# VectorE's low halves of v, cut into single turns and spread over step 0, in a masked attention kernel

## The chip, the cores and the metric

The kernel runs on one core of a Trainium2 chip. The metric is the device time of one execution in microseconds (us); lower is better. The engines are TensorE (PE in the profile), VectorE (DVE), ScalarE (ACT), GpSimd (POOL) and SyncE (SP), which here only issues transfers.

## The reference

With M = N = 6144 and D = 128, x goes through a layer norm and a relu, is multiplied by a 128x128 weight and by the transposed nodes, is masked by an adjacency matrix, goes through a softmax over the 6144 nodes, and the result weighs the nodes:

```python
h = jnp.maximum(_layernorm(x, axis=-1), 0.0)
anchor_adj = jnp.einsum('md,de,ne->mn', h, weight, input)
scores = jnp.where(adj > 0, anchor_adj, NEG_PAD)
atten = jax.nn.softmax(scores / TEMPERATURE, axis=1)
x = x + atten @ input
```

## The kernel before, in words

The rows of x are done in 48 tiles of 128. One step t of the main loop does the second half of the work of tile t and, interleaved with it, the scores of tiles t+1 and t+2. A tile's 6144 columns are cut into 12 "turns" of 512. For each turn k, the probabilities are transposed and split in a high and a low fp16 half, and `product(t, par, k, at)` multiplies them with `v`, the nodes, which are held as two fp16 halves too: `v[:, block, 0, :]` is the high half and `v[:, block, 1, :]` the low one. A turn has four blocks of 128 nodes (PER_TURN = 4), and `v` has 48 blocks.

`v` is made once. The high halves are made by ScalarE (L474) in four parts of 12 blocks, that is of three turns each (PART = 12 blocks, PART_TURNS = 3). The low half is `nodes * scale - high`. Parts 0 and 3 (turns 0 to 2 and 9 to 11) are made by GpSimd, each by two instructions (L397, then L400), and parts 1 and 2 (turns 3 to 5 and 6 to 8) by VectorE with one `scalar_tensor_tensor` each (L649), which reads the raw nodes and the high half, both in SBUF. VectorE's two fall in step 0, at the middle of its first and of its second cycle.

A step has three cycles z, each of four turns. Every engine runs a program of its own, written out by hand, and waits on semaphores. The orders that matter here are these.

- TensorE, in each cycle: transposes of turn 4z (L795, function `turn`), six score matmuls of one 1024-column chunk (L777), transposes of turn 4z+1, products of turns 4z and 4z+1 (L819 and L821, eight matmuls a turn), six more score matmuls, in cycle 0 the transposes of h of tile t+2 (L770), and products of turns 4z+2 and 4z+3. In step 0 the score chunks are chunks 4 and 5 of tile 1, then 0 to 3 of tile 2.
- VectorE, in each cycle: two low halves of turns that were transposed by DMA (`lo_d`, L611), the low half of turn 4z (`lo_p`, L605), the masking and the running maximum of one score chunk (`mask`, L583), `lo_p` of turn 4z+1, in cycle 1 also the statistics of x (L562, L565), and a second `mask`. Behind the second one in cycle 0 come the low half of h (`lo_h`, L569) and `find_max` (L591, L593).
- ScalarE: the high half of the transposed turn (`hi_p`, L487), an exponential of 1024 columns (L446), two of 512 (L455) and their high halves (`hi_d`, L467), some of which wait for DMA transposes.
- GpSimd: for every 2048 columns of the adjacency one `present` (L375) and one `absent` (L384), and per tile three small operations for the layer norm (L354, L357, L363). Its part 3 of v (L397, L400) lies between the absent of tile 2's first columns and the present of its second.

A turn's transposes go into one of three PSUM banks; `turn` waits on `turn_freed` until the low half that read that bank is done. So turn 5 waits for the first `lo_d` of cycle 1. Product k needs the low halves of v for its turn in step 0 only; every later step uses them as they are.

Of the kernel before, what the change touches and what calls it, by code (L numbers as in the profile page):

```python
# [5 lines left out]
def gnn_masked_attention_kernel(  # L6
# [29 lines left out]
    PER_TURN = TURN // P  # L36
# [9 lines left out]
    PART = BLOCKS // PARTS  # L46
    PART_TURNS = TURNS // PARTS
# [28 lines left out]

    EARLY = 4

    V_POOL = (0, 3)
    V_VECTOR = (1, 2)  # L80
    HEAD = 3
    TAIL = 5

# [9 lines left out]
    with ctx:  # L93
# [6 lines left out]
        def sem(name):  # L100
            return ctx.enter_context(nc.semaphore(name))
# [110 lines left out]
        v_hi_done = sem("v_hi_done")  # L212
        v_lo_done = sem("v_lo_done")
# [25 lines left out]
        def evac(t, n, at=None):  # L239


            if at == LAST and n >= 8:
                n -= 2
            return t * TURNS + (n + 1 + EARLY)

        def high(t, n, at=None):

            return t * TURNS + (n - CYCLE + 3 + EARLY) if at == LAST and n >= 0 else evac(t, n)
# [9 lines left out]
        def has(at, ahead):  # L258
            return at is None or at + ahead < TILES
# [82 lines left out]
        def _(pool):  # L342
# [48 lines left out]
            def v_lo_pool(n):  # L391

                i = V_POOL[n]
                blocks = slice(i * PART, (i + 1) * PART)
# [164 lines left out]
        def _(dve):  # L559
# [13 lines left out]
            def mask(u, s, j):  # L573
                if isinstance(u, int) and u == 1 and j // PER_CONV == 1:
                    dve.wait_ge(absent_early_done, 1)
                elif isinstance(u, int) and (u == 0 or u == 1 and j < PER_CONV):
                    dve.wait_ge(absent_done, u * CONVS + (j // PER_CONV + 1))
                else:
                    dve.wait_ge(absent_done, u * CONVS + j // PER_CONV)
                dve.wait_ge(scores_made, u * SCORES + (j + 1))  # L580
                dve.sem_inc(dve_waited, 1)
                c, part = j // PER_CONV, j % PER_CONV
                nc.vector.tensor_tensor_reduce(  # L583
                    out=probs[:, s, j * SCORE:(j + 1) * SCORE],
                    in0=ps_s[j % 2][:, :], in1=absent[:, c, part * SCORE:(part + 1) * SCORE],
                    scale=1.0, scalar=LOWEST, op0=ALU.subtract, op1=ALU.max,
                    accum_out=chunk_max[:, s, j:j + 1]).then_inc(masked, 1)
# [8 lines left out]
            def lo_p(t, k, at):  # L596
                n, p = k, P_TURN[k]
                if at == LAST:
                    dve.wait_ge(turned, t * P_TURNS + (p + 1))
                    dve.wait_ge(pv_done, t * TURNS + (MULTIPLIED[p - BANKS] + 1 - (0 if p >= BANKS else TURNS)))  # L600
                    nc.vector.tensor_copy(pT_hi[:, p % BANKS, :], ps_t[n % BANKS][:, :]).then_inc(last_hi_done, 1)  # L601
                    dve.wait_ge(last_hi_done, p + 1)
                else:
                    dve.wait_ge(hi_done, evac(t, n, at))
                nc.vector.tensor_tensor(pT_lo[:, p % BANKS, :], ps_t[n % BANKS][:, :], pT_hi[:, p % BANKS, :],  # L605
                                        ALU.subtract).then_inc(turn_freed, 1)

            def lo_d(c, g, n, count):
                d = c + g
                dve.wait_ge(hi_done, count)  # L610
                nc.vector.tensor_tensor(split[:, d % BANKS, 1, :], ps_t[n % BANKS][:, :], split[:, d % BANKS, 0, :],  # L611
                                        ALU.subtract).then_inc(turn_freed, 1)
# [11 lines left out]
            def finish(u, s, free):  # L624
                dve.wait_ge(inv_done, u + 1)
                dve.wait_ge(x_res_in[s], loads(u, s))
                dve.wait_ge(pv_done, u * TURNS + TURNS)
                nc.vector.scalar_tensor_tensor(out=fin_a[:, s, :], in0=ps_o[:, 0:D], scalar=inv_sum[:, s, :],
                                               in1=x_res[:, s, :], op0=ALU.mult, op1=ALU.add)\
                    .then_inc(fin_a_done, 1)  # L630
                dve.wait_ge(fin_a_done, u + 1)
                if free:
                    dve.wait_ge(stored[s], loads(u - 2, s))
                nc.vector.scalar_tensor_tensor(out=fin[:, s, :], in0=ps_o[:, D:2 * D], scalar=inv_sum[:, s, :],
                                               in1=fin_a[:, s, :], op0=ALU.mult, op1=ALU.add)\
                    .then_inc(fin_done, 1)
# [5 lines left out]
                                               in1=yT_hi[:, cols], op0=ALU.mult, op1=ALU.subtract)\  # L642
                    .then_inc(y_lo_done, 1)

            def v_lo(i):
                dve.wait_ge(v_hi_done, i + 1)
                dve.wait_ge(scale_steps, 4)
                blocks = slice(i * PART, (i + 1) * PART)
                nc.vector.scalar_tensor_tensor(out=v[:, blocks, 1, :], in0=nodes_raw[:, blocks, :], scalar=scale,  # L649
                                               in1=v[:, blocks, 0, :], op0=ALU.mult, op1=ALU.subtract)\  # L650
                    .then_inc(v_lo_done, 1)
# [79 lines left out]
            mask(1, 1, 2)  # L731
            mask(1, 1, 3)

            def step(t, par, at):
                nxt = 1 - par
                if at != 0:
                    finish(t - 1, nxt, at is None or at > 2)
                for z in range(CYCLES):

                    ahead, c = ((0, 2), (0, 4), (1, 0))[z]  # L740
                    if has(at, ahead):
                        for g in range(2):
                            n = CYCLE * z - 2 + g
                            lo_d(c, g, n, high(t, n, at))
                    lo_p(t, CYCLE * z, at)
                    for q in range(2):
                        ahead, j = S_AT[CYCLE * z + 2 + q]
                        if has(at, ahead):
                            mask(t + ahead, (par + ahead) % 2, j)
                            if j == SCORES - 1:  # L750
                                if has(at, 2):
                                    lo_h(t + 2, par, ps_s[0])
                                find_max(t + ahead, (par + ahead) % 2)
                        if q == 0:
                            lo_p(t, CYCLE * z + 1, at)
                            if z == 1 and has(at, 3):
                                x_stats(t + 3, nxt)
                            if z == 2:
                                invert_sum(t, par)
                            if at == 0 and z < 2:  # L760
                                v_lo(V_VECTOR[z])

            steps(dve, step)
            finish(TILES - 1, (TILES - 1) % 2, True)

        @block.tensor
        def _(pe):
# [29 lines left out]
                made.then_inc(turned, 1)  # L797

            def product(t, par, k, at):
                if at == 0 and k % PART_TURNS == 0:  # L800
                    part = k // PART_TURNS
                    if part in V_POOL:
                        pe.wait_ge(v_lo_pool_done, V_POOL.index(part) + 1)
                    else:
                        pe.wait_ge(v_lo_done, V_VECTOR.index(part) + 1)
                if k in MULTIPLIED:
                    p = MULTIPLIED.index(k)
                    pe.wait_ge(turn_freed, evac(t, k - 2, at))
                    hi = [pT_hi[:, p % BANKS, b * P:(b + 1) * P] for b in range(PER_TURN)]
                    lo = [pT_lo[:, p % BANKS, b * P:(b + 1) * P] for b in range(PER_TURN)]  # L810
                else:
                    d = k // CYCLE * 2 + k % 2
                    pe.wait_ge(turned_in[d], t * 16 + 16)
                    hi = [pT_dma[:, d, b, :] for b in range(PER_TURN)]
                    lo = [pT_dma[:, d, PER_TURN + b, :] for b in range(PER_TURN)]
                area = ps_o
                for b in range(PER_TURN):
                    blk = k * PER_TURN + b
                    nc.tensor.matmul(area[:, 0:2 * D], hi[b], v[:, blk, :, :].rearrange("p s d -> p (s d)"),  # L819
                                     start=(blk == 0), stop=(blk == BLOCKS - 1), skip_group_check=True)  # L820
                    made = nc.tensor.matmul(area[:, 0:D], lo[b], v[:, blk, 0, :],  # L821
                                            start=False, stop=(blk == BLOCKS - 1), skip_group_check=True)
                made.then_inc(pv_done, 1)
# [112 lines left out]
```

## Time and profile before

| what | value |
|---|---|
| median of 3 executions | 939.33 us |
| lowest and highest | 935.38 and 939.46 us |
| the profiled execution's own time | 936.15 us |
| its span in the profile | 934.2 us |
| PE busy | 915.2 us (98%) |
| DVE busy | 814.7 us (87%) |
| ACT busy | 757.8 us (81%) |
| POOL busy | 656.7 us (70%) |

Busy time is that of the profiled execution, over its span. Matmuls overlap in the pipeline, so a busy PE does not mean one at its peak. Step 0 begins at about 41 us and ends at about 66 us of the span.

### The profile page before, as it was taken

How to read it: one execution, taken by the hardware profiler on the slowest of the kernel's cores; microseconds unless marked ns; L12 is line 12 of the kernel's file. 1: busy time of each engine (PE TensorE's matmuls, PEld its weight loads, DVE VectorE, ACT ScalarE, POOL GpSimd, SP SyncE). 2: the span in 40 equal slices, each digit the busy share in tenths (PEclk: the TensorE clock that was granted, in tenths of full speed). 3: DMA queues.
4: the chain of work that ended last, by engine and by line, in shares of the span. 5: the costliest groups of instructions: out<-in, count | busy, mean ns of one | idle time of the engine just before them, and what ended most of it. 6: DMA issues, size and time to landing. Idle time of an engine off the chain costs nothing.

```text
span 934.2 us, 25959 instructions
## 1 busy us (share of the span) xinstructions
PE 915.2 (98%) x7611; PEld 664.6 (71%) x7611; DVE 814.7 (87%) x1675; ACT 757.8 (81%) x1512; POOL 656.7 (70%) x443
## 2 busy tenths in 40 slices
PE   7989999999999999999999999999999999999997
PEld 4457777777777777777777777777777777777776
DVE  7888888888888889888888889888888888888886
ACT  6868788888888888888888888888888888888885
POOL 4999677767767776777677767776777677767710
PEclk9999999999999999999999999999999999999999
DMA  9799999999999999999999999999999999999955
GB/s 338 239 221 250 274 271 263 269 260 266 264 269 266 260 262 267 269 266 257 267 269 268 251 269 267 274 249 270 270 265 257 263 273 265 264 260 260 271 94 97
DMA packets 347401, 239.51 MB, mean 256 GB/s; under 512 B 308848, under 2 KB 327408, under 8 KB 328944
## 3 DMA queue, kind: packets, MB, share of 16 engines
q1 hardware_dynamic: 340176, 235.92, 97.2%
q10 hardware_dynamic: 7200, 3.28, 1.2%
q8 instruction: 13, 0.21, 0.1%
q14 instruction: 12, 0.10, 0.0%
HBM read 160.50 MB, written 3.15 MB: 175 GB/s over the span
## 4 chain that ended last, share of the span: by engine, by line
PE 93%; DVE 3%; DMA 2%; ACT 1%; issue 1%; DVEq 0%; SPq 0%; ACTq 0%
PE ps_s L777 38%; PE ps_o L819 26%; PE ps_t L795 13%; PE ps_o L821 13%; DMA pT_dma<-split 1%; DVE probs L583 1%; PE ps_t L838 1%; PE ps_s L848 1%; DVE pT_lo L605 1%; PE ps_s L770 1%; DMA nodes_raw<-in_L_gnn_input_dram 1%; DVE split L611 0%; DVE v L649 0%; ACT ps_t L455 0%; DVE pT_hi L601 0%
## 5 line engine op out<-in xcount | busy, mean ns | idle before, releaser
L583 DVE CUSTOM_DVE_ANT_0 probs<-ps_s,absent 128x1024 f32<-128x1024 f32 x288 | 351.6, 1221 | 80.6 <-PE ps_s L777 58.2
L384 POOL TENSOR_SCALAR absent<-present 128x2048 bf16<-128x2048 bf16 x143 | 299.5, 2094 | 79.3 <-DVE chunk_max L583 53.4
L375 POOL TENSOR_SCALAR present<-adj_i 128x2048 bf16<-128x2048 int32 x144 | 274.6, 1907 | 28.9 <-DMA adj_i<-in_adj_dram 23.8
L487 ACT ACTIVATE pT_hi<-ps_t 128x512 f16<-128x512 f32 x282 | 168.3, 597 | 113.9 <-PE ps_t L795 111.3
L455 ACT ACTIVATE ps_t<-probs,neg_max,exp_scale 128x512 f32<-128x512 f32 x288 | 222.9, 774 | 2.9 <-DVE neg_max L593 1.2
L777 PE MATMUL ps_s<-yT_hi,hT_hi 128*128 128x512 f16 x576 | 218.3, 379 | 1.1 <-DVE chunk_max L583 0.9
L777 PE MATMUL ps_s<-yT_lo,hT_hi 128*128 128x512 f16 x576 | 218.2, 379 | 0.0
L819 PE MATMUL ps_o<-v,pT_hi 128*128 128x256 f16 x1152 | 207.3, 274 | 5.1 <-DVE v L649 3.7
L819 PE MATMUL ps_o<-v,pT_dma 128*128 128x256 f16 x1152 | 205.6, 273 | 0.0
L605 DVE TENSOR_TENSOR pT_lo<-ps_t,pT_hi 128x512 f16<-128x512 f32 x288 | 196.9, 684 | 3.4 <-ACT pT_hi L487 3.2
L821 PE MATMUL ps_o<-v,pT_lo 128*128 128x128 f16 x1152 | 199.2, 220 | 0.0
L821 PE MATMUL ps_o<-v,pT_dma 128*128 128x128 f16 x1152 | 197.9, 219 | 0.0
L611 DVE TENSOR_TENSOR split<-ps_t,split 128x512 f16<-128x512 f32 x288 | 185.2, 682 | 5.2 <-ACT split L467 5.0
L467 ACT ACTIVATE split<-ps_t 128x512 f16<-128x512 f32 x288 | 162.2, 589 | 21.7 <-DMA pT_dma<-split 20.5
L795 PE MATMUL ps_t<-ident,probs 128*128 128x128 f32 x1152 | 175.9, 276 | 3.5 <-DVE split L611 3.5
L446 ACT ACTIVATE probs<-probs,neg_max,exp_scale 128x1024 f32<-128x1024 f32 x144 | 177.7, 1234 | 0.0
L777 PE MATMUL ps_s<-yT_hi,hT_lo 128*128 128x512 f16 x576 | 171.3, 379 | 0.0
L795 PEld LDWEIGHTS ps_t<-ident,probs 128*128 128x128 f32 x1152 | 128.7, 141 | 40.3 <-DVE split L611 20.4
L819 PEld LDWEIGHTS ps_o<-v,pT_hi 128*128 128x128 f16 x1152 | 113.1, 98 | 32.9 <-DVE v L649 4.4
L821 PEld LDWEIGHTS ps_o<-v,pT_lo 128*128 128x128 f16 x1152 | 113.1, 98 | 11.4
L819 PEld LDWEIGHTS ps_o<-v,pT_dma 128*128 128x128 f16 x1152 | 112.7, 98 | 11.5
L821 PEld LDWEIGHTS ps_o<-v,pT_dma 128*128 128x128 f16 x1152 | 112.7, 98 | 1.6
(72 smaller groups left out, 590.1 us busy)
## 6 DMA issues: line engine op xcount, KB each, us to landing
adj_i<-in_adj_dram SPq DMA_DIRECT2D x144, 1024.0 KB, 5.1
pT_dma<-split SPq DMA_TRANSPOSE x288, 3.4
nodes_raw<-in_L_gnn_input_dram SPq DMA_DIRECT2D x6, 512.0 KB, 7.0
x_res<-in_x_dram SPq DMA_DIRECT2D x48, 64.0 KB, 4.7
out_dram<-fin ACTq DMA_DIRECT2D x48, 64.0 KB, 2.9
x_ln<-in_x_dram SPq DMA_DIRECT2D x46, 64.0 KB, 4.9
x_ln<-in_x_dram ACTq DMA_DIRECT2D x2, 64.0 KB, 3.4
w<-in_L_gnn_weight_dram SPq DMA_DIRECT2D x1, 64.0 KB, 2.1
```

The source lines that it names most:

```text
L375: nc.gpsimd.tensor_scalar(flags(s, c), adj_i[:, c, :], 1.0, 0.0, ALU.min, ALU.max)\
L384: nc.gpsimd.tensor_scalar(by_block(absent[:, c, :]), by_row(flags(s, c)), -ABSENT, ABSENT, ALU.mult, ALU.add).then_inc(absent_done, 1)
L446: nc.scalar.activation(part, part, ACT.Exp, bias=neg_max[:, s, :], scale=exp_scale[:, :], accum_out=chunk_sum[:, s, c // 2:c // 2 + 1]).th ...
L455: nc.scalar.activation(ps_t[n % BANKS][:, :], probs[:, s, col:col + TURN], ACT.Exp, bias=neg_max[:, s, :], scale=exp_scale[:, :], accum_ou ...
L487: nc.scalar.activation(pT_hi[:, p % BANKS, :], ps_t[k % BANKS][:, :], ACT.Copy).then_inc(hi_done, 1)
L583: nc.vector.tensor_tensor_reduce(out=probs[:, s, j * SCORE:(j + 1) * SCORE], in0=ps_s[j % 2][:, :], in1=absent[:, c, part * SCORE:(part + ...
L605: nc.vector.tensor_tensor(pT_lo[:, p % BANKS, :], ps_t[n % BANKS][:, :], pT_hi[:, p % BANKS, :], ALU.subtract).then_inc(turn_freed, 1)
L611: nc.vector.tensor_tensor(split[:, d % BANKS, 1, :], ps_t[n % BANKS][:, :], split[:, d % BANKS, 0, :], ALU.subtract).then_inc(turn_freed, 1)
L777: made = nc.tensor.matmul(ps_s[j % 2][:, q * 512:(q + 1) * 512], part[:, s, :], y[:, cols], start=(part is hT_hi and y is yT_hi), stop=(pa ...
L795: made = nc.tensor.transpose(ps_t[k % BANKS][:, b * P:(b + 1) * P], probs[:, par, col:col + P], ident[:, :])
L819: nc.tensor.matmul(area[:, 0:2 * D], hi[b], v[:, blk, :, :].rearrange("p s d -> p (s d)"), start=(blk == 0), stop=(blk == BLOCKS - 1), ski ...
L821: made = nc.tensor.matmul(area[:, 0:D], lo[b], v[:, blk, 0, :], start=False, stop=(blk == BLOCKS - 1), skip_group_check=True)
```

## The change

VectorE's two instructions of 12 blocks each become six of 4 blocks, one for each of the turns 3 to 8. `V_VECTOR` now maps a place (cycle, place in the cycle) to turns. Place 0 is behind the first `lo_p` of a cycle, place 1 behind the second one (and the statistics, where the instruction stood before), and place 2 behind the second `mask` and what follows it. Turn 3 comes at place 1 of cycle 0, turn 4 at place 2 of cycle 0, turns 5, 6 and 7 at places 0, 1 and 2 of cycle 1, and turn 8 at place 0 of cycle 2. `product` waits in front of each turn of step 0, where it waited in front of every third one, and for a turn of VectorE's it waits for that turn's instruction alone.

```diff
-    V_VECTOR = (1, 2)
+    V_VECTOR = {(0, 1): (3,), (0, 2): (4,), (1, 0): (5,), (1, 1): (6,), (1, 2): (7,), (2, 0): (8,)}
+    FIRST_V_VECTOR = 3
...
-            def v_lo(i):
-                dve.wait_ge(v_hi_done, i + 1)
+            def v_lo(k):
+                dve.wait_ge(v_hi_done, k // PART_TURNS + 1)
                 dve.wait_ge(scale_steps, 4)
-                blocks = slice(i * PART, (i + 1) * PART)
+                blocks = slice(k * PER_TURN, (k + 1) * PER_TURN)
...
+            def early_v_lo(at, z, place):
+                if at == 0:
+                    for k in V_VECTOR.get((z, place), ()):
+                        v_lo(k)
+
...
                     lo_p(t, CYCLE * z, at)
+                    early_v_lo(at, z, 0)
...
                             if z == 2:
                                 invert_sum(t, par)
-                            if at == 0 and z < 2:
-                                v_lo(V_VECTOR[z])
+                            early_v_lo(at, z, 1)
+                        else:
+                            early_v_lo(at, z, 2)
...
             def product(t, par, k, at):
-                if at == 0 and k % PART_TURNS == 0:
+                if at == 0:
                     part = k // PART_TURNS
                     if part in V_POOL:
                         pe.wait_ge(v_lo_pool_done, V_POOL.index(part) + 1)
                     else:
-                        pe.wait_ge(v_lo_done, V_VECTOR.index(part) + 1)
+                        pe.wait_ge(v_lo_done, k - FIRST_V_VECTOR + 1)
```

## Rows read from the trace of the kernel before

**Rows 1.** The page: its first line, and a group of section 5.

```profile
span 934.2 us, 25959 instructions
...
L819 PE MATMUL ps_o<-v,pT_hi 128*128 128x256 f16 x1152 | 207.3, 274 | 5.1 <-DVE v L649 3.7
```

**Rows 2.** Windows of one step's length: busy us of each engine, granted clock, DMA.

```profile
302.50:320.90 18.40, 18.40 (x157) 13.49 (x156) 16.21 (x35) 15.31 (x32) 13.29 (x10) 1.00 1.02 265
```

**Rows 3.** The timeline of TensorE in step 0: start, length, idle before.

```profile
48.44 0.28 PE L819 MATMUL ps_o<-v,pT_hi 128*128 128x256 f16 x1 [1.34 <-DVE v L649]
...
49.11 0.61 PE L795 MATMUL ps_t<-ident,probs 128*128 128x128 f32 x4
49.88 0.38 PE L777 MATMUL ps_s<-yT_hi,hT_hi 128*128 128x512 f16 x1 [0.16 <-DVE hT_lo L569]
...
51.17 0.60 PE L795 MATMUL ps_t<-ident,probs 128*128 128x128 f32 x4
51.60 0.27 PE L819 MATMUL ps_o<-v,pT_dma 128*128 128x256 f16 x1
...
56.70 0.29 PE L819 MATMUL ps_o<-v,pT_hi 128*128 128x256 f16 x1 [2.31 <-DVE v L649]
...
59.13 1.06 PE L795 MATMUL ps_t<-ident,probs 128*128 128x128 f32 x4
...
61.85 0.27 PE L819 MATMUL ps_o<-v,pT_dma 128*128 128x256 f16 x1
```

**Rows 4.** The timeline of VectorE in step 0.

```profile
46.58 1.81 DVE L649 SCALAR_TENSOR_TENSOR v<-nodes_raw,scale_bits,v 128x1536 f16<-128x1536 f32 x1
48.30 1.22 DVE L583 CUSTOM_DVE_ANT_0 probs<-ps_s,absent 128x1024 f32<-128x1024 f32 x1
...
49.96 1.28 DVE L611 TENSOR_TENSOR split<-ps_t,split 128x512 f16<-128x512 f32 x2
...
51.75 1.22 DVE L583 CUSTOM_DVE_ANT_0 probs<-ps_s,absent 128x1024 f32<-128x1024 f32 x1
...
54.04 2.60 DVE L649 SCALAR_TENSOR_TENSOR v<-nodes_raw,scale_bits,v 128x1536 f16<-128x1536 f32 x1
56.56 1.21 DVE L583 CUSTOM_DVE_ANT_0 probs<-ps_s,absent 128x1024 f32<-128x1024 f32 x1
...
57.70 1.28 DVE L611 TENSOR_TENSOR split<-ps_t,split 128x512 f16<-128x512 f32 x2
```

**Rows 5.** The timeline of GpSimd before and in step 0.

```profile
37.29 3.12 POOL L400 TENSOR_TENSOR v<-nodes_raw,v 128x1536 f16<-128x1536 f32 x1
...
46.68 3.63 POOL L384 TENSOR_SCALAR absent<-present 128x2048 bf16<-128x2048 bf16 x1 [0.21 <-POOL present L375]
50.28 1.56 POOL L397 TENSOR_SCALAR nodes_raw<-nodes_raw,scale_bits 128x1536 f32<-128x1536 f32 x1
51.92 3.10 POOL L400 TENSOR_TENSOR v<-nodes_raw,v 128x1536 f16<-128x1536 f32 x1
54.99 3.40 POOL L375 TENSOR_SCALAR present<-adj_i 128x2048 bf16<-128x2048 int32 x1
...
60.59 1.89 POOL L375 TENSOR_SCALAR present<-adj_i 128x2048 bf16<-128x2048 int32 x1
62.71 2.05 POOL L384 TENSOR_SCALAR absent<-present 128x2048 bf16<-128x2048 bf16 x1 [0.22 <-POOL present L375]
...
65.11 0.57 POOL L357 TENSOR_TENSOR rstd<-var_eps,minus_half 128x1 f32<-128x1 f32 x1
```

**Rows 6.** The timeline of ScalarE in step 0.

```profile
49.01 0.60 ACT L467 ACTIVATE split<-ps_t 128x512 f16<-128x512 f32 x1 [1.76 <-DMA pT_dma<-split]
...
51.80 0.60 ACT L487 ACTIVATE pT_hi<-ps_t 128x512 f16<-128x512 f32 x1 [0.23 <-PE ps_t L795]
```

**Rows 7.** The timeline of VectorE ahead of step 0: the same operation on 512 columns.

```profile
19.13 0.74 DVE L641 SCALAR_TENSOR_TENSOR yT_lo<-ps_t,y_scale_bits,yT_hi 128x512 f16<-128x512 f32 x1
```

**Rows 8.** Windows of 1 us for TensorE alone: busy us, granted clock, DMA.

```profile
57.00:58.00 1.00, 1.00 (x8) 0.50 0.00 0
```

## The prediction

> **What bounds the kernel now.** I read the page first, then windows of a step's length, then step 0 engine by engine. The page shows a span of 934.2 us and, in the group of the products, 3.7 us in which TensorE sat idle for VectorE's low halves of v (L649) [rows 1]. A window of 18.4 us from the middle has TensorE busy for all of it, the others at 16.2, 15.3 and 13.3 us, at full clock [rows 2]. So after step 0 TensorE sets the pace, and what step 0 gains or loses at its end should arrive at the end of the kernel nearly whole. The whole question is when TensorE reaches the products of turn 8, at 61.85 us before [rows 3].
>
> In step 0 the products of turn 3 waited 1.34 us for L649, those of turn 6 2.31 us [rows 3]. Behind the second wait the granted clock stood at 0.50, that is 1.2 in place of 2.4 GHz [rows 8]. The two turns of products behind it took 2.43 us (56.70 to 59.13), where one took 0.67 us at full clock (48.44 to 49.11). From there to turn 8 it took 2.72 us, where two transposes of 0.43 us (51.17 to 51.60) and six score matmuls of 1.29 us (49.88 to 51.17) give 2.15. So the low clock cost (2.43 - 1.34) + (2.72 - 2.15) = 1.7 us [rows 3].
>
> **What one small instruction costs.** The same operation on 512 columns took 0.74 us [rows 7], and a 1536-column one 1.81 us [rows 4]: 1.07 us for 1024 columns. The next instruction of VectorE started 1.72 us after the first L649 [rows 4], so 1.72 - 1.07 = 0.65 us for 512. Six cost 3.9 us of VectorE where two cost 3.4: 0.5 us more, in an engine that has idle time later. [...]
>
> **What the rows show of VectorE and GpSimd.** This decides the case. L400 took 3.10 us with the second L649 issued inside it, as it did alone (3.12), but that L649 took 2.60 us instead of 1.81 and ended at 56.64 us, 1.65 us after the next GpSimd instruction was issued at 54.99 [rows 4, 5]. That next one, L375, took 3.40 us instead of 1.89. In front of it L384, issued 0.10 us after the first L649, took 3.63 instead of 2.05 us [rows 5]. So the two engines don't run together here: whichever begins first holds the other off for its whole length, and a waiting VectorE gets in ahead of GpSimd's next instruction. L649 is the only one that reads two SBUF operands; the masks ran beside GpSimd at 1.21 to 1.22 us each.
>
> What no row shows is a one-input GpSimd instruction (L375, L384) that holds L649 off, since the two times that it could have, L649 came first. The bounds are nothing and the whole rest of that instruction. I take the whole, since those same instructions were held off by L649, so they use what it uses. The Trainium skill ("SBUF — State Buffer", section "SBUF: two separate sides") says that such a VectorE operation and a GpSimd one take an exclusive lock for the whole instruction, first come, first served, and that the other blocks; the L400 rows agree, and by this rule too the sum below is the one that holds.
>
> **Step 0 under that reading.** The lengths when VectorE has waited, again minus 1.07 us: done 1.65 - 1.07 = 0.58 us after it gets in, next VectorE instruction after (56.56 - 54.99) - 1.07 = 0.50, GpSimd held for (3.40 - 1.89) - 1.07 = 0.44 us [rows 4, 5].
>
> - Turn 3. L649 starts at 46.58 as before, done at 47.32. Its products start at 47.37 instead of 48.44: 1.07 us gained. The mask and all behind it move forward by the same.
> - Turn 4. VectorE is ready at 49.96 - 1.07 = 48.89. L384 now ends at 46.68 + 3.63 - 1.07 = 49.24, so it waits 0.35 us; done at 49.82, next at 49.74. The first `lo_d` (0.68 us) ends at 50.42 and releases turn 5's transposes, at 50.47 instead of 51.17. Products of turn 4 at 50.90, over at 51.57. Its second split from ScalarE is there at 49.61 [rows 6].
> - Turn 5. VectorE's three low halves take 1.79 us (49.96 to 51.75) [rows 4]: ready at 51.53. GpSimd: 49.24 + 0.44 + 1.56 + 0.08 puts L400's start at 51.32. So L400 is under way by 0.2 us, and holds VectorE until 51.32 + 3.07 = 54.39. Done at 54.97, products at 55.02 instead of 51.60 + 0.67 = 52.27. The gain has become a loss of 2.8 us, and TensorE has been idle for 3.45 us.
> - Turn 6. From 54.89, mask, `lo_p` and statistics take 2.29 us (51.75 to 54.04): ready at 57.18. GpSimd's L375 runs to 54.39 + 0.44 + 1.89 = 56.72, L384 from 56.94 to 58.99. VectorE gets in at 58.99, done at 59.57. Products at 59.62 instead of 56.70.
> - Turn 7. A mask of 1.14 us (56.56 to 57.70) from 59.49: ready at 60.63. L375 runs from 58.99 + 0.44 to 61.32. Done at 61.90, products at 61.95 to 62.62 (before: to 59.13).
> - Turn 8. Turn 8's transposes at 62.62, ScalarE's half starts 0.63 us later (51.17 to 51.80) and takes 0.60, `lo_p` 0.60: ready at 64.45. GpSimd: L384 from 61.76 to 63.81, and 0.35 us later (65.11 - 62.71 - 2.05) L357, 64.16 to 64.73. Done at 65.31, products at 65.36.
>
> That is 65.36 - 61.85 = 3.5 us later than before, with TensorE at full clock. It waits in front of turns 5, 6, 7 and a little 8. What is queued behind each waiting L649 is VectorE's mask and its low halves, and behind TensorE's wait its scores; that is in the sum. GpSimd is not late at the end: its L357 comes at 64.16 instead of 65.11. The DMA transposes and the adjacency loads have no new wait in front of them.
>
> **The clock.** It fell before after a wait of 2.31 us and cost 1.7 us. Now TensorE waits 3.45 us once and 2 us more, so a fall is likely. Its cost is hidden as long as TensorE waits anyway for turns 6 and 7, and shown behind 61.95. I take half of the 1.7, 0.8 us; bounds: nothing, and the next but one rival. Sum: 3.5 + 0.8 = 4.3 us slower. Against the profiled execution's own 936.15 us that is 940.5; that execution lies 3.2 us under the median of its runs, and against the median, 939.33 us, I forecast 943.6 us, range of this case 942.8 (no fall) to 944.5 (all of the 1.7).
>
> **The rivals.**
>
> 1. *No hold-off by one-input GpSimd instructions, or turn 5's instruction slips in before L400.* In the first, only L400 costs: turn 5 done at 54.55, turn 6's ready at 56.8, products at 57.6, turn 7's at 59.3, turn 8's at 62.6: 0.8 us slower. In the second, turn 5's products come at 52.3, L400 runs to 55.2 and holds turn 6's (products 55.8), L375 holds turn 7's (58.1) and turn 8's (62.5): 0.7 us slower. For it: the margin is 0.2 us in a sum of ten terms. Against: both sides hang on the same end of L384 at 49.24, so it moves little. 940.1 us.
> 2. *No hold-off at all*: the change does what it is cut for. Turn 5's products at 52.1, turn 6's at 55.1, turn 7's at 56.9, turn 8's at 60.1: 1.7 us faster, 937.6 us. For it, the waits of 1.34 and 2.31 us are real. Against it, the second L649's 2.60 us.
> 3. *The clock stays at half until turn 8 and past it.* The other side of the bound for a change. From 61.95: products 1.22 us, transposes 0.86 twice, scores 2.58, and the products of turns 8 and 9 2.43, over at 69.9; before they were over at 61.85 + 1.34 = 63.2. 6.7 us slower, 946.0 us. It decides when the low clock costs over 1.2 us behind 61.95 (3.5 + 1.2 = 4.7). For it: more idle time, in more pieces, than before. Against it: before, with TensorE busy from 56.70 on, the product at 61.85 took 0.27 us again, as at full clock at 51.60 [rows 3].
>
> **How the numbers follow.** 0.5% of 939.33 is 4.7 us, about what a measurement can tell from no change (the three runs themselves span 4.1 us). Chances: my forecast 0.40, rival 1 0.20, rival 2 0.13, rival 3 0.22, something else 0.05. Rival 3 is slower by over 0.5%, with a fifth of my own forecast's chance, which lies at that edge (0.08), and a little of the rest: 0.31. Faster by over 0.5% needs a gain that no case gives: 0.04. Within 0.5%: 0.65. The range goes from rival 2, 937.6, to just over rival 3, 946.5; the runs' own scatter leaves the rest outside.
>
> **What the profile after would show.** Right: six L649, the first near 0.74 us, turn 5's near 3.4 us and ending just behind L400, those of turns 6 and 7 at 1 to 2.4 us, each ending about 0.6 us after a GpSimd instruction ends; TensorE's waits on v at 7 us and more in place of 3.7; turn 8's products near 65 us. All six at 0.74 us would be rival 2; only turn 5's long, rival 1. A granted clock of 0.50 behind 62 us measures rival 3. I am wrong if step 1 or later takes up the delay, or if turn 5 gets in before L400.

## The result, and the profile after

The changed kernel takes 941.7 us at the median of 22 executions (939.1 to 944.2), the kernel before 938.05 us at the median of 22 (935.2 to 940.7). The ratio is 1.0044, with a 95% interval of 1.0036 to 1.0053: about 4.1 us slower; the two medians by themselves differ by 3.65 us. The forecast was 4.3 us slower. In absolute terms it was 943.6 us, set against a median of three executions of before, 939.33 us; the measured 941.7 lies within the whole range given (937.6 to 946.5), but under the 942.8 to 944.5 of the forecast's own case. The profiled execution of the changed kernel has a span of 938.9 us, 4.7 us more than the one of before [rows 1].

The page of the changed kernel: its first line and the two groups of the products.

```profile
span 938.9 us, 25975 instructions
...
L828 PE MATMUL ps_o<-v,pT_hi 128*128 128x256 f16 x1152 | 206.3, 273 | 5.7 <-DVE v L651 4.2
L828 PE MATMUL ps_o<-v,pT_dma 128*128 128x256 f16 x1152 | 206.8, 274 | 1.3 <-DVE v L651 1.3
```

TensorE waits 5.5 us (4.2 + 1.3) for the low halves of v where it waited 3.7 [rows 1], and it waits still more by another route, as the timeline of TensorE shows (start, length, idle before):

```profile
48.79 0.28 PE L828 MATMUL ps_o<-v,pT_hi 128*128 128x256 f16 x1 [1.24 <-DVE v L651]
...
54.53 1.12 PE L804 MATMUL ps_t<-ident,probs 128*128 128x128 f32 x4 [2.85 <-DVE split L613]
...
60.71 0.28 PE L828 MATMUL ps_o<-v,pT_hi 128*128 128x256 f16 x1 [1.39 <-DVE v L651]
...
63.15 0.28 PE L828 MATMUL ps_o<-v,pT_hi 128*128 128x256 f16 x1 [1.61 <-DVE v L651]
...
67.42 0.28 PE L828 MATMUL ps_o<-v,pT_dma 128*128 128x256 f16 x1 [1.26 <-DVE v L651]
```

The transposes of turn 5 at 54.53 wait for a split of VectorE that stands behind the low half of turn 4, so those 2.85 us belong to v as well: 8.35 us in all. Turn 8's products come at 67.42 instead of 61.85 [rows 3]. The cause is in the timelines of VectorE, and then of GpSimd:

```profile
46.96 1.78 DVE L651 SCALAR_TENSOR_TENSOR v<-nodes_raw,scale_bits,v 128x512 f16<-128x512 f32 x1
...
50.31 3.56 DVE L651 SCALAR_TENSOR_TENSOR v<-nodes_raw,scale_bits,v 128x512 f16<-128x512 f32 x1
...
55.60 0.74 DVE L651 SCALAR_TENSOR_TENSOR v<-nodes_raw,scale_bits,v 128x512 f16<-128x512 f32 x1
...
58.53 2.13 DVE L651 SCALAR_TENSOR_TENSOR v<-nodes_raw,scale_bits,v 128x512 f16<-128x512 f32 x1
...
61.72 1.37 DVE L651 SCALAR_TENSOR_TENSOR v<-nodes_raw,scale_bits,v 128x512 f16<-128x512 f32 x1
...
65.70 1.66 DVE L651 SCALAR_TENSOR_TENSOR v<-nodes_raw,scale_bits,v 128x512 f16<-128x512 f32 x1
```

```profile
46.15 2.04 POOL L386 TENSOR_SCALAR absent<-present 128x2048 bf16<-128x2048 bf16 x1 [0.22 <-POOL present L377]
...
50.23 3.10 POOL L402 TENSOR_TENSOR v<-nodes_raw,v 128x1536 f16<-128x1536 f32 x1
...
58.22 1.89 POOL L377 TENSOR_SCALAR present<-adj_i 128x2048 bf16<-128x2048 int32 x1
60.33 2.22 POOL L386 TENSOR_SCALAR absent<-present 128x2048 bf16<-128x2048 bf16 x1 [0.22 <-POOL present L377]
...
64.92 1.89 POOL L377 TENSOR_SCALAR present<-adj_i 128x2048 bf16<-128x2048 int32 x1
```

The same 512-column operation takes 0.74 us once and 1.37 to 3.56 us five times. Start plus length gives the ends of the five: 48.74, 53.87, 60.66, 63.09 and 67.36 us. Each is 0.54 or 0.55 us after the end of the GpSimd instruction that was under way when it was issued (48.19, 53.33, 60.11, 62.55 and 66.81). Here the first of them was issued 0.81 us behind GpSimd's L386, where its counterpart in the kernel before came 0.10 us ahead of it [rows 4, 5], and everything behind it met GpSimd at other points than in the forecast.

Such a shift can be seen 30 us ahead of step 0. The timelines of VectorE and GpSimd of the changed kernel:

```profile
15.18 1.75 DVE L659 TENSOR_TENSOR y_bound<-nodes_top,w_top 128x1 f32<-128x1 f32 x1
```

```profile
15.03 1.90 POOL L377 TENSOR_SCALAR present<-adj_i 128x2048 bf16<-128x2048 int32 x1 [6.78 <-DMA adj_i<-in_adj_dram]
```

and VectorE's of the kernel before:

```profile
15.40 0.16 DVE L657 TENSOR_TENSOR y_bound<-nodes_top,w_top 128x1 f32<-128x1 f32 x1
```

`y_bound` multiplies one element per partition by another, both in SBUF. In the changed kernel's profile it ended with GpSimd's first instruction on the adjacency (15.18 + 1.75 = 15.03 + 1.90), 1.6 us later than its own length asks for. This line is the same in both kernels; it is a matter of which of them comes first. That it decides the order in step 0 is inferred, but the 13 profiles of this case agree. In five of them (this one and those of experiments 1, 2, 8 and the second run of 4) y_bound ended 1.5 to 1.9 us after that GpSimd instruction was issued, and the first low half was issued 0.48 to 0.81 us behind GpSimd's absent. In seven it ended at most 1.01 us after it, and the low half was issued 0.10 or 0.11 us ahead. In the last, that of experiment 10, GpSimd was made to wait.

### The profile page after: what moved, and what is told of

Same layout as the page of the kernel before. It is cut to its first block, busy times and chain, and to the rows that moved or that the text cites. A ratio compares the mean times of both kernels' runs of the same rounds, so it can differ in the third digit from the quotient of the medians.

```text
span 938.9 us, 25975 instructions
## 1 busy us (share of the span) xinstructions
PE 915.9 (98%) x7611; PEld 665.0 (71%) x7611; DVE 822.5 (88%) x1679; ACT 760.8 (81%) x1512; POOL 655.6 (70%) x443
## 4 chain that ended last, share of the span: by engine, by line
PE 94%; DVE 3%; ACT 1%; issue 1%; DMA 1%; SPq 0%; DVEq 0%; ACTq 0%
PE ps_s L786 39%; PE ps_o L828 26%; PE ps_t L804 13%; PE ps_o L830 13%; DVE probs L585 1%; PE ps_t L847 1%; PE ps_s L857 1%; DVE v L651 1%; PE ps_s L779 1%; DVE pT_lo L607 0%; DMA nodes_raw<-in_L_gnn_input_dram 0%; DVE split L613 0%; DMA pT_dma<-split 0%; ACT ps_t L457 0%; DVE pT_hi L603 0%
## 5 line engine op out<-in xcount | busy, mean ns | idle before, releaser
L386 POOL TENSOR_SCALAR absent<-present 128x2048 bf16<-128x2048 bf16 x143 | 298.7, 2089 | 76.4 <-DVE chunk_max L585 51.1
L377 POOL TENSOR_SCALAR present<-adj_i 128x2048 bf16<-128x2048 int32 x144 | 273.8, 1902 | 34.1 <-DMA adj_i<-in_adj_dram 30.4
L469 ACT ACTIVATE split<-ps_t 128x512 f16<-128x512 f32 x288 | 164.8, 589 | 23.1 <-DMA pT_dma<-split 20.9
```

Source lines behind the costliest of these rows:

```text
L377: nc.gpsimd.tensor_scalar(flags(s, c), adj_i[:, c, :], 1.0, 0.0, ALU.min, ALU.max)\
L386: nc.gpsimd.tensor_scalar(by_block(absent[:, c, :]), by_row(flags(s, c)), -ABSENT, ABSENT, ALU.mult, ALU.add).then_inc(absent_done, 1)
```

## The experiments

Ten kernels were run, one of them twice. Ratios are to the kernel before, on the same chip, with 95% intervals. Theory A is the prediction's: the two engines hold each other off. Theory B is that more instructions and waits, or their new places, cost the time by themselves.

**1. One SBUF operand in place of two, the change as it is.** The subtraction of the high half is left out.

```diff
-                nc.vector.scalar_tensor_tensor(out=v[:, blocks, 1, :], in0=nodes_raw[:, blocks, :], scalar=scale,
-                                               in1=v[:, blocks, 0, :], op0=ALU.mult, op1=ALU.subtract)\
+                nc.vector.tensor_scalar(v[:, blocks, 1, :], nodes_raw[:, blocks, :], scale, -1.0,
+                                        ALU.mult, ALU.mult)\
```

> The changed kernel, with VectorE's six low halves made by an operation that reads one SBUF operand (the scaled nodes alone; the subtraction of the high half is left out, so v's low half holds the wrong values). Same 512 columns, same places, same semaphores. Theory A (VectorE and GpSimd hold each other off where VectorE reads two SBUF operands): all six take about 0.74 us whatever GpSimd does, GpSimd's instructions beside them keep their 1.9 to 2.1 us, TensorE hardly waits on v, and the kernel is about 1.7 us faster than the kernel before (ratio 0.998) and 5 to 6 us faster than the changed one. Theory B (more instructions, more waits and the new places cost the time, not the hold-off): it stays slower than before by about 4 us (ratio 1.004).

Measured: 940.84 us, ratio 1.0028 (1.0013 to 1.0043). A miss for theory A as written. Its timeline of VectorE says why:

```profile
50.11 3.31 DVE L651 TENSOR_SCALAR v<-nodes_raw,scale_bits 128x512 f16<-128x512 f32 x1
...
55.14 0.47 DVE L651 TENSOR_SCALAR v<-nodes_raw,scale_bits 128x512 f16<-128x512 f32 x1
```

Where nothing held it, it took 0.47 us for 512 columns, not 0.74: faster than the rows of before allow for one column at a time (1024 columns more cost 1.07 us there, so 512 cost 0.53). And it was held like the original (3.31 us). So this kernel did not take the conflict away, and its time parts no theories. The Trainium skill ("SBUF — State Buffer", section "Who interferes with whom") lists this operation among those that can run in a two-port mode and then contend with GpSimd, and `tensor_reduce` as one that never does on this chip. The trace agrees: 0.47 us and held here, 0.68 us and not held in experiment 6. That gave experiments 6 and 7.

**2. The same in the kernel before.**

> The kernel before, with its two low halves of 1536 columns made by the same one-operand operation (subtraction left out, wrong values in v's low half). Theory A: both take about 1.8 us, the second no longer 2.6, GpSimd's L384 and L375 beside them stay at 1.9 to 2.1 us instead of 3.4 to 3.6; 0.8 us of the second wait goes and part of the low clock's 1.7 us with it: 0.8 to 2 us faster than before (ratio 0.998 to 0.999), and less good than the six, which also win the 1 us of turn 3. Theory B: no difference to the kernel before.

Measured: 934.1 us, ratio 0.9956 (0.9941 to 0.9970). Faster than theory A's 0.998, but for another reason in part. The 1536 columns would need only about 1.0 us; this is an estimate: held, they ended 0.82 us behind GpSimd's instruction, 512 columns of experiment 1 0.28 us behind, so 1024 more cost 0.54 on top of 0.47. And both were still held (2.14 and 1.65 us). It shows that shorter low halves help; it doesn't part the theories.

**3. The cut without the new places.**

```diff
+    V_VECTOR = {(0, 1): (3, 4, 5), (1, 1): (6, 7, 8)}
```

> The changed kernel with the six instructions back to back, three at each of the two places of before: the cut alone, without the new places. Theory A: a GpSimd instruction that waits can get in between two of the three and hold the next for up to 2 us; otherwise as before, with turn 3 1.07 us earlier. Between 1 us faster and 2 us slower than before (0.999 to 1.002), so at least 2 us better than the changed kernel. Theory B with the number of instructions as cause: as slow as the changed kernel (1.004). Theory B with the places as cause: as before (1.000).

Measured: 940.99 us, ratio 1.0027 (1.0014 to 1.0041): 2.5 us slower than before, a little outside the range given for theory A, and by the ratios 1.6 us better than the changed kernel where at least 2 were expected. The timelines of VectorE and of GpSimd:

```profile
45.98 5.12 DVE L651 SCALAR_TENSOR_TENSOR v<-nodes_raw,scale_bits,v 128x512 f16<-128x512 f32 x3
...
58.00 5.49 DVE L651 SCALAR_TENSOR_TENSOR v<-nodes_raw,scale_bits,v 128x512 f16<-128x512 f32 x3
```

```profile
46.09 2.53 POOL L386 TENSOR_SCALAR absent<-present 128x2048 bf16<-128x2048 bf16 x1 [0.22 <-POOL present L377]
48.60 1.97 POOL L399 TENSOR_SCALAR nodes_raw<-nodes_raw,scale_bits 128x1536 f32<-128x1536 f32 x1
```

Three back to back took 5.12 us where 0.65 + 0.65 + 0.74 = 2.04 would do. GpSimd gets in between each two of them, and each time it costs a whole GpSimd instruction: the three end at 51.10, 0.53 us behind L399's end (50.57). One instruction of 1536 columns is held once; three of 512 can be held three times. Here the cut loses without any new place. Its ratio alone fits theory B's number of instructions nearly as well; it is the lengths in the timeline that speak for the hold.

**4. y_bound without a second SBUF tensor, in the kernel before.**

```diff
-                nc.vector.tensor_tensor(y_bound[:, :], nodes_top[:, :], w_top[:, :], ALU.mult)\
+                nc.vector.tensor_scalar(y_bound[:, :], nodes_top[:, :], w_top[:, :], None, ALU.mult)\
```

> The kernel before, where y_bound (128x1, ahead of everything: the product of two maxima) is made with one of them as a scalar operand instead of by an operation on two SBUF tensors. In the changed kernel's profile this one-element operation took 1.75 us, 15.18 to 16.93, exactly to the end of GpSimd's first instruction on the adjacency; in the profile of before it started 0.09 us ahead of that instruction and took 0.16. Theory A: it now takes 0.16 us in every execution, and the scatter of 935 to 940 us closes at its fast end: median 936 us, ratio 0.998. Rival (the 1.75 us is something else, or is hidden later): ratio 1.000 and the same scatter.

Measured: 934.33 us (934.0 to 935.3), ratio 0.9955 (0.9938 to 0.9971), better than expected. It was run again later:

> The kernel before with y_bound alone changed, once more, beside the fenced one on the same chip: 934.3 us, ratio 0.995 to 0.997. If the fences matter, this one has the wider scatter of the two.

Measured: 935.53 us (933.6 to 939.4, 12 executions), ratio 0.9981 (0.9965 to 0.9998). So the gain is real, 2 to 4 us, but the scatter does not close (5.8 us). In this second profile y_bound took 0.21 us, and yet the first L649 was held:

```profile
46.71 3.16 DVE L649 SCALAR_TENSOR_TENSOR v<-nodes_raw,scale_bits,v 128x1536 f16<-128x1536 f32 x1
```

It was issued 0.49 us behind GpSimd's L384 (46.22). Here y_bound was late by itself, issued at 16.41, 1.32 us behind GpSimd's first instruction. So it can still come late without being held, and its new form only shifts the odds.

**5. The same y_bound in the changed kernel.**

> The changed kernel with y_bound made as in the run before (one maximum as a scalar operand), so that step 0 is entered early and alike in every execution. The same for the kernel before gave 934.3 us, its first low half of v issued at 46.11, 0.11 us ahead of GpSimd's L384. Theory A: here the prediction's own sequence should be seen (turn 3 free, turn 5 held to the end of L400's counterpart near 53.9, turns 6 to 8 held by one-input GpSimd instructions): 3.5 us over 934.3, that is 937.8, ratio to the kernel before 0.999. If GpSimd's L384 gets in first instead, turn 3 is held as well and it is 5 us: 939.3 us, ratio 1.001. Theory C (the change itself costs little, the loss was y_bound being held more often in the changed kernel): 934 to 935 us, ratio 0.996.

Measured: 941.13 us, ratio 1.0042 (1.0018 to 1.0067). Slower than the expected 937.8 us by 3.3 us, with the expected sequence, which its timeline of VectorE shows:

```profile
46.05 0.74 DVE L651 SCALAR_TENSOR_TENSOR v<-nodes_raw,scale_bits,v 128x512 f16<-128x512 f32 x1
...
48.37 0.89 DVE L651 SCALAR_TENSOR_TENSOR v<-nodes_raw,scale_bits,v 128x512 f16<-128x512 f32 x1
...
50.98 3.42 DVE L651 SCALAR_TENSOR_TENSOR v<-nodes_raw,scale_bits,v 128x512 f16<-128x512 f32 x1
...
56.60 2.33 DVE L651 SCALAR_TENSOR_TENSOR v<-nodes_raw,scale_bits,v 128x512 f16<-128x512 f32 x1
...
59.99 1.23 DVE L651 SCALAR_TENSOR_TENSOR v<-nodes_raw,scale_bits,v 128x512 f16<-128x512 f32 x1
...
64.86 0.74 DVE L651 SCALAR_TENSOR_TENSOR v<-nodes_raw,scale_bits,v 128x512 f16<-128x512 f32 x1
```

The prediction had, for the same six, 0.74, 0.93, 3.44, 2.39, 1.27 and 0.86 us, and its starts are 0.52 to 0.64 us later than the first five of these, evenly, as step 0 itself is entered 0.53 us earlier here. The sixth comes 0.41 us later than predicted, so about 1 us was lost on VectorE between the fifth and the sixth. There the clock had fallen once more, as windows of TensorE show (window, its length, busy us, granted clock, DMA):

```profile
60.00:62.00 2.00, 0.72 (x5) 0.75 0.23 82
62.00:64.00 2.00, 2.00 (x11) 0.50 0.44 87
```

The profile of experiment 4 has the same entry into step 0, the same wait of 2.31 us in front of turn 6 as before, and no fall of the clock behind it. Its timeline and windows of TensorE, then the products of turn 8 in experiment 5:

```profile
56.23 0.28 PE L819 MATMUL ps_o<-v,pT_hi 128*128 128x256 f16 x1 [2.31 <-DVE v L649]
...
59.73 0.27 PE L819 MATMUL ps_o<-v,pT_dma 128*128 128x256 f16 x1
```

```profile
56.00:58.00 2.00, 1.77 (x21) 1.00 0.00 0
58.00:60.00 2.00, 2.00 (x15) 1.00 0.56 106
```

```profile
65.66 0.28 PE L828 MATMUL ps_o<-v,pT_dma 128*128 128x256 f16 x1
```

So turn 8 comes 5.9 us later with the change than without it here (65.66 - 59.73). In the profile of before TensorE needed 5.15 us from the first product of turn 6 to that of turn 8 (56.70 to 61.85), with the clock down; in experiment 4's it needed 3.50. So 1.65 of the 5.9 us are low clock that the kernel without the change does not have here, and that the forecast's 61.85 contained. The rest, 4.3 us, is what the prediction had.

**6 and 7. tensor_reduce in place of the low half, with y_bound as above: six, and two.** The scaling and the subtraction are left out.

```diff
+                nc.vector.tensor_reduce(v[:, blocks, 1, :], nodes_raw[:, blocks, :].rearrange("p b (d o) -> p b d o", o=1),
+                                        AX.X, ALU.max)\
```

> As after_with_bound, but VectorE's six instructions are tensor_reduce over an axis of length 1: one SBUF operand, one element per cycle, same size, places and semaphores (scaling and subtraction are left out, v's low half holds the nodes themselves). In one_input_six the replacement ran 512 columns in 0.47 us, two per cycle, so it used both of VectorE's ports and was held as before; this one should not be. Theory A: all six at 0.7 us whatever GpSimd does, GpSimd's instructions at 1.9 to 2.1 us, TensorE hardly waits on v: 1.7 us under 934.3, 932.6 us, ratio 0.994. Theory B (the cut and its places cost by themselves): like after_with_bound.

> The kernel before with y_bound as above and its two 1536-column low halves made by the same tensor_reduce (scaling and subtraction left out). Theory A: both at 1.8 us, the second not at 2.6, GpSimd beside them not stretched to 3.4 and 3.6. TensorE's second wait 1.5 instead of 2.3 us; 0.8 us and a part of the low clock if it then stays up: 933 to 933.6 us, ratio 0.995, and the six are 0.5 to 1.5 us better than the two, which is what the cut would be worth without the hold-off. Theory B: 934.3 us.

Measured: six 933.9 us, ratio 0.9959 (0.9938 to 0.9980); two 932.81 us, ratio 0.9948 (0.9927 to 0.9968). The timelines of VectorE and of GpSimd with six:

```profile
50.96 0.68 DVE L651 TENSOR_REDUCE v<-nodes_raw 128x512 f16<-128x512 f32 x1
53.82 0.69 DVE L651 TENSOR_REDUCE v<-nodes_raw 128x512 f16<-128x512 f32 x1
```

```profile
50.10 3.12 POOL L402 TENSOR_TENSOR v<-nodes_raw,v 128x1536 f16<-128x1536 f32 x1
53.19 1.90 POOL L377 TENSOR_SCALAR present<-adj_i 128x2048 bf16<-128x2048 int32 x1
```

At the same place as in experiment 5, in the middle of L402, the low half of turn 5 takes 0.68 us instead of 3.42, and the one behind it, in the middle of a one-input L377, takes 0.69. Places, sizes, count and semaphores are those of the changed kernel; 7.2 us are gone (941.13 to 933.9). A part of them comes by way of the clock: its mean is 1.000 in this profile and 0.996 in experiment 5's. An instruction is also 0.06 us shorter, and v's low half holds other numbers, which has not been tested by itself. But none of this accounts for 3.42 against 0.68 us at the same place, and theory B is out. But the second half of the expectation failed: the six are not better than the two, they are 1.1 us slower. In the two profiles 0.64 us of that is there before the first low half (46.32 against 45.68), so not much more than half a microsecond can be laid to the cut. It won nothing even without GpSimd.

**8 and 9. GpSimd's part 3 of v, one conversion later, with y_bound as above: in the kernel before, and in the changed one.**

```diff
             convert(2, 0, 0, True)
-            v_lo_pool(1)
...
                     convert(t + 2, par, 1, True)
+                    if at == 0:
+                        v_lo_pool(1)
```

> The kernel before with y_bound as above, and GpSimd's low half of v's part 3 (L397 and the two-input L400, 4.7 us) moved behind its next conversion, into step 0. Theory A: the second low half on VectorE now meets the end of a 2 us instruction in place of the 3.1 us one, held for about 0.5 instead of 0.8 us; part 3 is ready near 60.4 us, just in time for turn 9: 934 us, ratio 0.995 to 0.996. If part 3 comes too late for turn 9, or the conversion behind it for the masks, 1 to 3 us are lost.

Measured: 934.07 us, ratio 0.9974 (0.9943 to 1.0005), but with one execution at 939.2. That is the profiled one, and both of its low halves were held (3.17 and 3.89 us). Where the others stood isn't known; no gain over y_bound alone can be told.

> The changed kernel with y_bound as above and GpSimd's part 3 of v behind its next conversion. It tells how much of the changed kernel's loss comes from the one long two-input instruction (L400's counterpart, 3.1 us) and how much from the 2 us one-input ones. Theory A: turn 5's low half, ready near 51.0 us, meets a one-input instruction about at its end and is held for under 0.5 us instead of 2.7; turns 6 and 7 then meet part 3's two instructions instead. Product 8 near 61.6 us instead of 66: 936.5 us (935 to 938), against 941.1 for the changed kernel with part 3 where it was. If only L400's place mattered and one-input instructions cost nothing, it would be 933 to 934 us.

Measured: 940.26 us, ratio 1.0023 (1.0007 to 1.0038), 3.8 us slower than expected. Turn 5's low half was free (0.74 us), but turns 6, 7 and 8 took 1.82, 2.43 and 0.91 us, TensorE waited 1.88 and 2.67 us for the first two of these, and then ran at a granted clock of 0.50 from 60 to 64 us. So L400's counterpart isn't the culprit alone: moving it moves the hold. The clock was still at 0.50 when turn 8 was reached: its first product took 0.42 us, at 65.08.

**10. GpSimd lets VectorE in first.**

```diff
-            convert(2, 0, 0, True)
+            find_present(2, 0, 0)
+            pool.wait_ge(v_lo_done, 1)
+            make_absent(2, 0, 0, True)
...
                     if at == 0:
+                        pool.wait_ge(v_lo_done, 2)
                         v_lo_pool(1)
```

> The version the experiments point to: the kernel before with y_bound without a second SBUF tensor, and with GpSimd made to let VectorE in first: its absent of tile 2 (L384) waits for VectorE's first low half of v, and its own part 3 of v stands one conversion later and waits for VectorE's second. Theory A: the first L649 takes 1.81 us in every execution, the second is held at most by the end of a one-input instruction (0 to 0.5 us), L400 never holds anyone: 933 to 934.3 us with little scatter, ratio to the kernel before 0.994 to 0.996. Rival: part 3, ready only near 61 us, or the conversion pushed behind it comes too late for turn 9 or the masks: 935 to 937 us.

Measured: 934.82 us (933.8 to 936.3, 10 executions), ratio 0.9966 (0.9953 to 0.9980), a little slower than expected. The first low half took 1.81 us, the second 2.35, so this one was still held for 0.54. It beats both kernels; against y_bound alone on the same chip (935.53) its median is 0.7 us lower, which the spread of that one (5.8 us) doesn't let one call a gain, but its own spread is 2.6 us. What the fences buy is that the order of the two engines no longer depends on who comes first at the first low half; that this is what narrows the spread is not shown.

## Why the prediction was right

**The hold-off, by two-input and one-input instructions alike: right, and shown.** The step that no row supported was that L375 and L384 hold L649 off as L400 does. In the profile after, four of the six end just over half a microsecond behind such a one-input instruction; experiment 6 takes the conflict away and keeps count, places and waits, and the 7.2 us go. Theory B, more instructions and more waits as such, would have stayed.

The extra waits of TensorE cost little: in front of the products of step 0 its queue shows six waits by themselves in the profile after (at L817) and two in that of before (at L808), of 0.051 us each, 0.2 us more at most.

**The sequence: right where step 0 is entered as in the profile of before, and not in the profile after.** Experiment 5 enters it so and repeats the six lengths within 0.12 us. The margin of 0.2 us by which L400 had to come first was 0.21 us there (50.77 and 50.98). In the profile of the changed kernel itself the entry was shifted, turn 4 instead of turn 5 met the 3.1 us instruction, and turn 3, forecast at 0.74 us, was held as well (1.78). The delay at turn 8 was then 5.6 us instead of 3.5 (67.42 - 61.85), and 4.7 us of it arrive in the span. By the start of ScalarE's operation on h in each step, the changed kernel is 5.6 us behind in steps 1 and 2, 4.3 in step 3, 5.0 from there on and 4.6 near the end, so most of it carries, as I had said, and 0.9 us are given back.

**The clock: the mis-sized term of the profile after.** I put it at 0.8 us. In the profile after, the clock fell while TensorE waited ahead of 54.53, the transposes there took 1.12 us, and it was back before 58 us; behind it TensorE waited 1.39 us for turn 6 anyway, so nothing of that shows at the end: 0 instead of 0.8. In experiment 5 it fell again, behind turn 6, where nothing covers it, and cost the 0.8 us of the forecast: with the entry 0.53 us earlier turn 8 should come at 64.83, and it came at 65.66. It was back by then (0.28 us for the first product), so this is not rival 3. Only experiment 9 had the low clock last until turn 8. The same wait of 2.31 us in front of turn 6 brought a fall in the profile of before and none in experiment 4's, so a wait's length by itself does not tell what the clock will cost here.

**The rivals.** Rival 2 (no hold-off) is what experiment 6 builds: 933.9 against 934.3 and 935.5 for the same kernel without the change, 0.4 to 1.6 us, where I had 1.7. These come from three chips; by the ratios it is from nothing to 2 us, and against experiment 7 the six lost 1.1. Rival 1's first half, no hold-off by one-input instructions, is out by the four holds. Its second half wanted turn 5 free of L400. In the profiled execution it was free, but because turn 4 had been held by L400's counterpart in its stead, which the rival had not foreseen.

**The sum: right in part by luck.** 4.3 us were forecast and the ratio gives 4.1. In the two profiles the parts differ more than the sum: 2.1 us more at turn 8 (5.6 for 3.5), 0.8 less for the clock and 0.9 given back make 4.7 of the 4.3. And the reckoning set one sequence of the change against one execution of before. The kernel before loses to the same conflict as well: with y_bound alone mended its medians are 934.33 and 935.53 instead of 938.05, and even then one profile has the first L649 held for 1.35 us.

That this is what scatters the executions of before is inferred, as only one of them was profiled. The record adds how the scatter goes: with the clock. Of the 52 executions of before that were run beside the experiments, the 20 with a mean granted clock of 0.996 took 938.9 us and more, the 28 with 0.998 took 934.8 to 938.8, the three with 1.000 934.9 to 935.7, and the one with 0.997 938.3. In the profiles 0.998 is one fall of the clock in step 0 and 1.000 is none.

With y_bound out of the way on both sides the change costs 5.6 to 6.8 us (941.13 against 935.53 and 934.33; by the ratios, which allow for the chip, 5.7 to 8.2). That this is near rival 3's 6.7 is chance. In the profiles of experiments 5 and 4 the difference at turn 8 is the forecast's 4.3 and the 1.65 us of low clock that the kernel without the change does not have there. By ScalarE's operation on h it is 5.4 us in step 2 and 6.65 from step 4 on, and by the spans 7.5 (939.6 and 932.1); what adds the rest is open.

## What to carry to other kernels

Before cutting a VectorE operation with two SBUF operands into smaller ones, look at what GpSimd does at each new place: every piece can be held for a whole GpSimd instruction, and the pieces can lose more than the one long wait that they replace. The sign in a timeline is one instruction whose length varies for the same shape and which ends a fixed time after the other engine's instruction ends. If a time scatters from execution to execution, look for the first place where two such instructions start within some tenths of a microsecond of each other, and at the granted clock of each execution.

## What was not expected of the hardware

A one-element operation on two SBUF tensors was held to the end of a one-input GpSimd instruction: 1.75 us in place of 0.16, and 1.03 and 0.77 us in experiments 1 and 2. With one of the two as a scalar operand it took 0.21 or 0.22 us in all eight profiles of the kernels that have it, seven times issued within that same GpSimd instruction, 0.12 to 1.35 us behind its start.

GpSimd, when it waits, gets in between two back-to-back operations of VectorE, as VectorE gets in between two of GpSimd's (experiment 3: 5.12 us for three).

`tensor_scalar` on 512 fp32 columns took 0.47 us and was held by GpSimd (3.31 us); `tensor_reduce` on the same columns took 0.68 and was not.
